# A fused attention and mixture kernel: fifteen of sixteen gate rows spread by transfer, logits, output norms and the first G product at other steps

## The reference

```
q, k, v = split(x @ Wqkv + bqkv);  q -= mean(q);  k -= mean(k)
q2 = l2norm_rows(q*q / (sum(q*q) + 1e-7));  k2 = l2norm_columns(k*k / (sum(k*k) + 1e-7))
x1 = layernorm(x + (v + q2 @ (k2.T @ v) / sqrt(1024)) @ Wln + bln)
sel = sigmoid(x1 @ expert_sel.T)                       # 16 gates for each token
z   = x1 + sum over e of sel[:, e] * (relu(x1 @ keys[e]) @ values[e])
out = layernorm(z)
```

## Time and profile before

| | us |
|---|---|
| median of 3 runs | 1011.67 |
| lowest, highest | 1010.37, 1012.95 |
| the profiled execution | 1008.1 |
| its span in the trace | 1006.1 |
| PE busy | 982.1 (98%) |
| VectorE busy | 805.2 (80%) |
| ScalarE busy | 526.9 (52%) |
| GpSimd busy | 55.1 (5%) |

### The profile page before, as it was taken

One profiled execution on the slowest core, in us unless ns is written; L12 is line 12 of the kernel. 1 busy time (PEld: TensorE's weight loads), 2 busy tenths in 40 slices (PEclk: granted clock), 3 DMA queues, 4 the chain that ended last, 5 costly groups with the idle time before them and its releaser, 6 DMA issues.

```text
span 1006.1 us, 20851 instructions
## 1 busy us (share of the span) xinstructions
PE 982.1 (98%) x7700; PEld 939.0 (93%) x7700; DVE 805.2 (80%) x1874; ACT 526.9 (52%) x1150; POOL 55.1 (5%) x75
## 2 busy tenths in 40 slices
PE   7899999999999999999999999999999999999996
PEld 6799999999999999999999999999999999999996
DVE  5889877888879887788878888788887888878545
ACT  4566544566355753556536565366644656454323
POOL 0010100101010010100101001010100101010100
PEclk8999999999999999999999999999999999999999
DMA  6054133352344323442333522425133352333221
GB/s 187 22 177 139 61 110 114 112 155 75 106 134 137 98 86 116 141 141 75 100 118 126 160 77 93 145 83 193 56 113 108 109 166 68 111 102 110 90 95 63
DMA packets 75624, 112.45 MB, mean 112 GB/s; under 512 B 7170, under 2 KB 37634, under 8 KB 75524
## 3 DMA queue, kind: packets, MB, share of 16 engines
q1 hardware_dynamic: 75524, 111.13, 34.3%
HBM read 87.51 MB, written 23.46 MB: 110 GB/s over the span
## 4 chain that ended last, share of the span: by engine, by line
PE 72%; DVE 12%; DMA 6%; issue 5%; ACT 3%; SPq 2%; POOL 0%; DVEq 0%; ACTq 0%; POOLq 0%
PE up_bank L1370 25%; PE down_bank L1370 25%; PE ring_bank L1370 9%; PE qk_bank L1370 7%; PE g_bank L1370 3%; DMA sel_all<-sel_out 3%; DVE gated_l L1113 2%; DMA parked_x<-w_room 2%; DVE gated L1131 2%; SPq L457 2%; DVE x1T_l L978 1%; DVE qk L1131 1%; ACT L646 1%; ACT z L721 1%; DVE z_stats L1075 1%
## 5 line engine op out<-in xcount | busy, mean ns | idle before, releaser
L1370 PE MATMUL down_bank<-vals_h,gated_h 128*128 128x256 f32 x1024 | 285.6, 279 | 4.9 <-DVE gated_l L1113 4.6
L1370 PE MATMUL down_bank<-vals_l,gated_h 128*128 128x256 f32 x1024 | 283.2, 277 | 0.0
L1370 PE MATMUL down_bank<-vals_h,gated_l 128*128 128x256 f32 x1024 | 283.2, 277 | 0.0
L1370 PE MATMUL up_bank<-x1T_l,keys_h 128*128 128x256 f32 (+1 forms) x928 | 267.7, 288 | 0.0
L1370 PE MATMUL up_bank<-x1T_h,keys_l 128*128 128x256 f32 (+1 forms) x928 | 267.7, 288 | 0.0
L1370 PE MATMUL up_bank<-x1T_h,keys_h 128*128 128x256 f32 (+1 forms) x928 | 267.6, 288 | 0.0
L578 ACT ACTIVATE gated_h<-gated 128x512 fp32r<-128x512 f32 x176 | 111.1, 631 | 196.4 <-DVE gated L1131 196.4
L1370 PEld LDWEIGHTS down_bank<-vals_h,gated_h 128*128 128x128 f32 x1024 | 192.3, 188 | 11.9 <-DVE gated_l L1113 7.6
L1370 PEld LDWEIGHTS down_bank<-vals_l,gated_h 128*128 128x128 f32 x1024 | 192.4, 188 | 4.1
L1370 PEld LDWEIGHTS down_bank<-vals_h,gated_l 128*128 128x128 f32 x1024 | 192.3, 188 | 0.0
L1131 DVE SCALAR_TENSOR_TENSOR gated<-up_bank,sel_all 128x512 f32<-128x512 f32 x176 | 121.3, 689 | 76.3 <-PE up_bank L1370 54.9
(11 more groups left out here) (259 smaller groups left out, 1774.4 us busy)
## 6 DMA issues: line engine op xcount, KB each, us to landing
sel_all<-sel_out SPq DMA_DIRECT2D x192, 256.0 KB, 3.8
out<-z SPq DMA_DIRECT2D x32, 256.0 KB, 2.5
x_raw<-in_x SPq DMA_DIRECT2D x15, 512.0 KB, 5.7
xT_raw<-in_xT SPq DMA_DIRECT2D x14, 512.0 KB, 5.6
parked_q<-w_room SPq DMA_DIRECT2D x14, 512.0 KB, 2.6
q<-parked_q SPq DMA_DIRECT2D x56, 128.0 KB, 3.0
parked_x<-w_room SPq DMA_DIRECT2D x14, 512.0 KB, 3.4
w_room<-parked_x SPq DMA_DIRECT2D x56, 128.0 KB, 3.0
```

The lines of the kernel that those rows point to most:

```text
L1370: last = mm(dst, lhs, rhs, start=start and i == 0, stop=stop and i == n - 1, **kw)
```

## The change

- The table: stage ZN of pairs 0 and 1 moves from steps 29 and 30 to steps 26 and 28, LG of half 0 from 30 to 29, the first G product from 9 to 10. (The steps 3 and 4, which have ZN for the other group, keep it, and `FIRST_PLAN` still has its first G product at 9.)
- Of each group but the very first, GpSimd spreads row 0 alone; rows 1 to 15 go through memory. The small transfer to `sel_rows` is left for the first group only.
- `move_rows` of half 1 stands at step 13 instead of 14.

```diff
--- before.py
+++ after.py
@@ -40,12 +40,12 @@
     plan={
         1: [], 2: [("ZA", 0), ("ZA", 1), ("Y", 4)], 3: [("ZN", 0), ("XS", 4)], 4: [("ZN", 1), ("Y", 5)],
         5: [("Y", 6), ("XS", 5)], 6: [("Y", 7), ("XS", 6)], 7: [("XS", 7), ("QK", 0)], 8: [("QK", 1)],
-        9: [("GG", 0)], 10: [("XR", 1), ("QK", 2), ("GG", 1)], 11: [("QK", 3), ("QS", 0)],
-        12: [("GG", 2), ("QK", 4), ("LG", 1), ("QS", 1)], 13: [("GG", 3), ("QS", 2)], 14: [("QK", 5), ("QS", 3)],
+        9: [], 10: [("XR", 1), ("QK", 2), ("GG", 0), ("GG", 1)],
+        11: [("QK", 3), ("QS", 0)], 12: [("GG", 2), ("QK", 4), ("LG", 1), ("QS", 1)], 13: [("GG", 3), ("QS", 2)], 14: [("QK", 5), ("QS", 3)],
         15: [("GG", 4), ("QK", 6), ("QS", 4)], 16: [("GG", 5), ("QS", 5)], 17: [("QK", 7)],
         18: [("ZA", 0), ("ZA", 1), ("QR", 0), ("GG", 6)], 19: [("KS", 0), ("GG", 7), ("QS", 6)], 20: [("KV", 0), ("QS", 7)],
         21: [("Y", 0)], 22: [("Y", 1), ("XS", 0)], 23: [("Y", 2), ("XS", 1)], 24: [("Y", 3), ("XS", 2)],
-        25: [("QR", 1), ("XS", 3)], 27: [("XR", 0)], 29: [("ZN", 0)], 30: [("LG", 0), ("ZN", 1)],
+        25: [("QR", 1), ("XS", 3)], 26: [("ZN", 0)], 27: [("XR", 0)], 28: [("ZN", 1)], 29: [("LG", 0)],
     },
 
 
@@ -62,12 +62,13 @@
 LAST = dict(plan={1: [("ZA", 0), ("ZA", 1), ("ZN", 0), ("ZN", 1)]}, split_xT={}, split_x={}, bias_x={},
             gpsimd_xT=(), gpsimd_x=())
 LAST_STEPS = 3
-ROWS_STEP = 14
+ROWS_STEP = 13
 WHOLE_UP = (0, 3, 20, 21, 25, 28)
 SPREAD = 4
 AHEAD = 3
 AHEAD_STEP = 27
-NEAR = 4
+NEAR_FIRST = 4
+NEAR = 1
 BLOCK = 32
 RING_KINDS = ("QT", "Y", "XT", "LG", "KS", "KV")
 
@@ -76,6 +77,21 @@
 PIECE_LO_STEPS = ((0, 2), (0, 3), (0, 5), (0, 6), (0, 9), (0, 10))
 PIECE_LOADS = ((0, 0), (0, 2), (0, 3), (0, 5), (0, 6))
 QUARTER = GN // 2
+
+
+def near(grp):
+
+    return NEAR if grp else NEAR_FIRST
+
+
+def near_made(grp):
+
+    return sum(near(g) for g in range(grp))
+
+
+def far_loads(f):
+
+    return sum(1 for n in range(f % SPREAD, f + 1, SPREAD) if n % E >= near(n // E))
 
 
 def batch_offset(kind, a):
@@ -461,10 +477,10 @@
 
                 grp = G * (it + off) + g
                 sp.wait_ge(sel_made, grp + 1)
-                at_least(sp, sel_spread, NEAR * grp)
-                sp.dma_start(sel_rows[0:P:32], sel[0:NEAR, :]).then_inc(rows_in, 16)
+                if grp == 0:
+                    sp.dma_start(sel_rows[0:P:32], sel[0:NEAR_FIRST, :]).then_inc(rows_in, 16)
                 at_least(sp, gate_applied, E * (grp - 1))
-                sp.dma_start(sel_out[g, NEAR:E], sel[NEAR:E, :]).then_inc(sel_written, 16)
+                sp.dma_start(sel_out[g, near(grp):E], sel[near(grp):E, :]).then_inc(sel_written, 16)
 
             def spread_far(f):
 
@@ -520,7 +536,7 @@
                         load_x_half(it, 0)
                 if s == AHEAD_STEP and has(it + 1, 1):
                     load_xT_half(it + 1, 0)
-                if step_exists(it, s + AHEAD) and (s + AHEAD) % E >= NEAR:
+                if step_exists(it, s + AHEAD) and (s + AHEAD) % E >= near((it * STEPS + s + AHEAD) // E):
                     spread_far(step_no(it, s + AHEAD))
                 if s == 5 and has(it, 1):
                     load_xT_half(it, 1)
@@ -551,7 +567,7 @@
             nc.gpsimd.memset(esel_hl[:].bitcast(F32), 0.0).then_inc(constants_set, 1)
 
             def spread_near(grp):
-                for e in range(NEAR):
+                for e in range(near(grp)):
 
                     at_least(pool, gate_applied, grp * E + e - SPREAD + 1)
                     if e == 0:
@@ -559,7 +575,7 @@
                         pool.wait_ge(sel_made, grp + 1)
                         row = sel[0:1, :]
                     else:
-                        pool.wait_ge(rows_in, 16 * (grp + 1))
+                        pool.wait_ge(rows_in, 16)
                         row = sel_rows[32 * e:32 * e + 1]
                     nc.gpsimd.partition_broadcast(sel_all[:, e], row, P).then_inc(sel_spread, 1)
 
@@ -704,10 +720,10 @@
                     elif kind == "LG":
                         act.wait_ge(logits_made, half(b, a))
 
-                        at_least(act, rows_in, 16 * (G * b + a))
+                        act.wait_ge(rows_in, 16)
                         at_least(act, sel_written, 16 * (G * b + a))
 
-                        at_least(act, sel_spread, NEAR * (G * b + a - 1) + 1)
+                        act.wait_ge(sel_spread, near_made(G * b + a - 1) + 1)
                         copy(sel[:], ring_of(it, s, kind, a)[LOW:LOW + E, :]).then_inc(logits_low, 1)
                     elif kind == "ZN":
                         n = out_pair(it, off, a)
@@ -1119,10 +1135,10 @@
                 if step_exists(it, s):
                     f = step_no(it, s)
                     dve.wait_ge(up_made, f + 1)
-                    if f % E < NEAR:
-                        dve.wait_ge(sel_spread, NEAR * (f // E) + f % E + 1)
+                    if f % E < near(f // E):
+                        dve.wait_ge(sel_spread, near_made(f // E) + f % E + 1)
                     else:
-                        dve.wait_ge(spread_in[f % SPREAD], 16 * ((E // SPREAD - 1) * (f // E) + f % E // SPREAD))
+                        dve.wait_ge(spread_in[f % SPREAD], 16 * far_loads(f))
 
                     if s == 19 and has(it, 1):
                         dve.wait_ge(q_fourth, k_tile(it + 1, T - 1))
```

## The result

The changed kernel takes 1021.73 us (median of 5, 1017.52 to 1022.19), the kernel before 1011.0 beside it (median of 5): 1.0095 times as long (95% interval 1.0073 to 1.0118). Measured once more, among the experiments, it took 1024.72 against 1010.04: 1.0146 (1.0128 to 1.0164). So it is slower by 10.7 us the first time and 14.7 the second; the forecast was 1025.5, or +13.9. The execution whose trace follows took 1021.73 us, 13.6 more than the one of before (1008.1).

A forecast was written before the change was run, and what follows sets the result against it. PE (TensorE), busy 98% of the span, was taken to bound the kernel, so only its waits count. +15.3 + 5.6 - 7.0 = +13.9 on the median 1011.7 gave 1025.6, said as 1025.5 us; range 1017 to 1034.

The forecast's parts named there:

- A: Step 29: PE waits for `x1T_l` before the earlier logits of half 0, in seven iterations; +15.3 us.
- B: Step 31: PE waits for `gated_l` because pair 0's store holds back gate row 30; +5.6 us (0 to 13.3).
- C: Steps 1 and 30: today's PE stalls for `gated_l` vanish; -7.0 us (between -5.6 and -7.5).
- Rows by transfer: 45 GpSimd broadcasts become transfers; rows land in time and VectorE is less disturbed; 0 to -0.5 us.
- First G product: Moved from step 9 to 10, it leaves the wait before `g_bank` at step 12; 0, with -2.4 as other end.
- No second wait: Rival: rows land in under 4.1 us, so no wait at step 31; +8.3 us, 1020; 25%.
- Longer landings: Rival: row 30 takes 5.9 us to land, B becomes 13.3; +21.6 us, 1033; 15%.
- Faster: Rival: turned tiles land before PE reaches the logits, only C is left; -7.0 us, 1004.7; 7%.
- nothing: Rival: no visible change, the wait before the logits about as long as C; 1012; 5%.
- The clock: Rival: each new idle piece of PE costs a 3.4 us stretch at half rate, 24 us more; 1050; 4%.

The follow-up runs named there:

- other_half: Changed kernel with the logits at step 29 computed from the turned x1 of half 1 instead of half 0 (half 0's gates wrong); 1024.96 us.
- norms_early: Changed kernel, half 0's logits back at step 30 and its rows 1 to 3 by GpSimd, pair 0's store behind rows 30 and 31; 1004.29 us.
- store_late: Changed kernel with the store of output pair 0 issued at step 28, behind the xT load and gate rows 30 and 31, instead of step 26; 1022.51 us.
- odd_rows: Kernel before with only half 1's rows, except the first, by transfer and written at step 13; 1007.07 us.
- filler: Changed kernel with twelve more matmuls of 256 columns, their result overwritten, ahead of the logits of step 29; 1021.01 us.
- load_late: Changed kernel, logits at 30, norms at 26 and 27, stores and xT load behind rows 30 and 31, half 0's rows 1 to 3 by GpSimd; 999.72 us.

## Why the prediction was right, point by point

- **A, +15.3: right in mechanism, place and size.** Over the plan, step 29 has 1.93, 1.92, 2.42, 1.97, 2.35, 4.21 and 1.81 us in the seven iterations, 16.6 together. The 4.21 holds part of a stretch at half rate; the waits alone are 15.5. The idle piece shown is 1.62 us where 1.66 was forecast. other_half took it away at its place, norms_early moved the logits back and the loss was gone.
- **B, +5.6: right in mechanism, and the size partly by luck.** Step 31 is 6.1 over the plan against 0.5 in before. It was 0.8 a piece in the forecast; the pieces are 0.91, 1.39, 0.78, 1.47, 0.50, 0.01, 0.67, so that one iteration has none and two have nearly twice as much. The landing, 5.2, was between the two that bounded it and not at the 4.7 that was taken. store_late removed the wait as the cause says.
- **C, -7.0: right in mechanism and within its bounds.** As waits, step 1 falls from 4.1 us to 0, step 2 from 1.9 to 1.6, step 30 from 1.7 to 0: -6.1, where the forecast allowed -5.6 to -7.5. (What step 30 still has over the plan in the changed kernel, 1.4, is 0.7 of the stretch at half rate and 0.7 of pace.) At step 1 the edit that was credited with norms and logits together needs only one of the two.
- **Rows by transfer, 0 to -0.5: the term that was mis-sized.** Steps 18 to 20, behind GpSimd's former broadcasts, have 2.5 us less of waits, 1.9 of them at step 20; the run that makes this edit for half 1 alone has 2.4 less there. I had looked for GpSimd's disturbance only where PE waited for `gated_l`, and took from one row that PE doesn't wait there. The place where it counted is the KV product at step 20, two links behind the disturbed instruction; its wait stands in the view of waits under "issue" (4.0 us), so that no releaser pointed there. Half 0's rows cost nothing that is seen: steps 2 and 3 are no longer than before.
- **First G product, 0: right.** The wait before `g_bank` is 2.4 us before and 2.5 after.
- **The sum.** As waits, 15.5 (A) + 5.2 (B) - 6.1 (C) - 2.5 (rows) = +12.1, as much as the waits of the loop grew by; 1.5 of clock and 0.8 of pace make it +14.4. The forecast was +13.9 without the rows' 2.5 and without clock and pace, 2.3: two omissions that nearly cancel, which is luck. The median came 3.8 under the 1025.5 the first time and 0.8 the second: the forecast put the difference of two executions onto a median whose own profiled execution had been 3.6 under it, and the changed kernel's was its median.
- **The rivals.** No second wait: out, B is there. Longer landings: out, 5.2 us and 5.6 for B, not 13.3. Faster and nothing: out. The clock: partly true. Behind the seven waits the changed kernel had one stretch at half rate in one trace and two in the other, and the price is 1.5 to 2.9 us, not 24. Two steps were wrong in it: a stretch at half rate loses half its length (some 15 matmuls, 1.5 to 1.7 us, of 3.4), and most of the idle pieces caused none. That the page's clock is 9 in every slice but the first, as forecast, doesn't exclude such a stretch: it is a small part of a slice of 25 us.

## What to carry over

When PE is full, an edit that puts its next matmul ahead of data that take a round trip through memory costs the whole distance, each time, and other waits hide behind that one: take one away and see which comes next before you count its gain. In a queue that issues in order, a store that waits for an instruction holds back every load behind it; put the loads that someone waits for ahead of it. Where a wait has no releaser, look at the producer's neighbours on all engines that were busy then.

## What the runs showed of the hardware

**The clock can fall after an idle piece of some 2 us amid full work, but doesn't each time.** Sums of stretches in the changed kernel, iteration 5 (start:end us, busy of each engine, then PEclk, DMA share); the idle piece before the logits there is 3.08 us, ending at 782.59:

```profile
780.50:784.00 3.50, 1.41 (x8) 1.26 (x9) 2.85 (x8) 2.89 (x7) 0.00 (x0) 1.00 0.17 62
784.10:787.30 3.20, 3.20 (x17) 3.20 (x16) 1.35 (x4) 3.16 (x5) 0.00 (x0) 0.50 0.88 271
787.50:791.00 3.50, 3.50 (x33) 3.50 (x32) 1.47 (x3) 1.27 (x3) 0.80 (x1) 1.00 0.36 126
```

PE works again for 1.4 us at full rate before the granted clock goes to 0.5 (1.2 GHz), does 17 matmuls in 3.2 us where the next 3.5 us have 33, and has the full rate (2.4 GHz) back at the next stretch. In all traces here it happened at or shortly behind sixteen idle pieces of the loop, from 1.98 us (other_half, at 299.63) to 3.08 (this one), and not at twelve of 1.96 to 3.10 (store_late, at 783.60), nor at any shorter one there. In before, odd_rows, norms_early, filler and load_late PE has no idle piece of 1.9 us or more in the loop and no such stretch, but for one at the loop's start in norms_early, behind pieces of 0.9 us with little work between. The length of the piece alone doesn't decide it; what does stays open.

**Matmuls in a row have two paces at the same granted clock.** Timeline of PE in load_late, twice, "..." for the matmuls between:

```profile
703.42 0.28 PE L1389 MATMUL up_bank<-x1T_h,keys_h 128*128 128x256 f32 x1
...
703.99 0.28 PE L1389 MATMUL up_bank<-x1T_h,keys_l 128*128 128x256 f32 x1
...
899.80 0.28 PE L1389 MATMUL up_bank<-x1T_h,keys_l 128*128 128x256 f32 x1
...
900.51 0.28 PE L1389 MATMUL up_bank<-x1T_h,keys_l 128*128 128x256 f32 x1
```

Five distances in 0.57 us, 0.114 each, and six in 0.71, 0.118 each, the clock being 1.00 in both stretches. The slower pace lasts from 850 to 958 us in this trace; in the kernel before it shows only for a few microseconds at a time (251.9 to 253.9, for one). The balance's column of pace, small change included, is 2.3 to 8.1 us. What causes it stays open; it is as large as most effects studied here, and a reason to compare two kernels by waits first.

**GpSimd's disturbance of VectorE shows in means, not only beside one broadcast**: 54 ns of 735 in the mean `x_l` between before and odd_rows. That edit as a whole gave 3.0 us by the medians and 2.4 us of waits at steps 18 to 20.
